# Three scatters behind each values step, and a wait for landings after each eighth

## What is computed

```python
x = x + _L0_xattn_ref(ctx_768, _layernorm(x, axis=-1), mask, ...)   # out = softmax(qn @ kn.T) @ v, then @ Wo.T + bo
x = x + _L0_ffn_ref(_layernorm(x, axis=-1), gate_w, gate_bias, w_gate, w_up, w_down)

# in _L0_ffn_ref, n = 4096 tokens, E = 64, K = 8, CAP = 256
scores = jax.nn.sigmoid(x @ gate_w.T)
topk_idx = jax.lax.top_k(tmp, K)[1]                       # tmp: scores + bias, within the best 4 groups
pos = jnp.take_along_axis(jnp.cumsum(oh, 0) - 1, e[:, None], 1)[:, 0]
buf = jnp.zeros((E, CAP + 1, h), x.dtype).at[e, pos_c].set(x[token])[:, :CAP]   # rows scattered to slots
g = jnp.einsum('ech,ehi->eci', buf, w_gate)
u = jnp.einsum('ech,ehi->eci', buf, w_up)
y = jnp.einsum('eci,eih->ech', jax.nn.silu(g) * u, w_down)
out = jnp.zeros((n, h), jnp.float32).at[token].add(y_slots * w_slot[:, None])
```

## Time and profile before

| | us |
|---|---|
| median of 3 runs | 1155.54 (1154.9 to 1157.93) |
| the profiled execution | 1165.68, its span 1163.8 |
| PE busy | 897.9 (77%) |
| VectorE busy | 660.5 (57%) |
| ScalarE busy | 463.1 (40%) |
| POOL busy | 616.1 (53%) |

### The profile page before, as it was taken

One profiled execution on the slowest core, in us unless ns is written; L12 is line 12 of the kernel. 1 busy time (PEld: TensorE's weight loads), 2 busy tenths in 40 slices (PEclk: granted clock), 3 DMA queues, 4 the chain that ended last, 5 costly groups with the idle time before them and its releaser, 6 DMA issues.

```text
span 1163.8 us, 13512 instructions
## 1 busy us (share of the span) xinstructions
PE 897.9 (77%) x3944; PEld 637.4 (55%) x3944; DVE 660.5 (57%) x1953; ACT 463.1 (40%) x931; POOL 616.1 (53%) x571
## 2 busy tenths in 40 slices
PE   2779999899999999989964974957209999888300
PEld 1445666556666657566642643856108888776200
DVE  4475657976888874978752644743623444333206
ACT  3834675645675546664530522422103333222000
POOL 4530323215766635755665063145555888888840
PEclk9969999989999999999985996968559999999655
DMA  7739601112222322101261102000518999898689
GB/s 249 269 100 386 232 5 53 38 31 105 80 73 76 125 68 88 65 7 68 79 230 65 37 28 88 24 23 9 205 67 252 308 313 182 160 162 138 71 237 385
DMA packets 85336, 150.79 MB, mean 130 GB/s; under 512 B 14089, under 2 KB 53049, under 8 KB 83215
## 3 DMA queue, kind: packets, MB, share of 16 engines
q1 hardware_dynamic: 54543, 112.32, 27.7%
q0 software_dynamic: 30720, 37.61, 16.3%
HBM read 69.19 MB, written 97.45 MB: 143 GB/s over the span
## 4 chain that ended last, share of the span: by engine, by line
PE 53%; DVE 13%; issue 10%; DMA 7%; POOL 6%; another core or an unknown queue 5%; ACT 5%; POOLq 0%; SPq 0%; DVEq 0%; ACTq 0%
PE ps_o L1302 15%; PE ps_u L1366 5%; PE ps_s L1278 4%; PE ps_u L1222 4%; PE ps_u L1192 4%; PE ps_s L1280 4%; POOL sum L1144 3%; DMA out_rows<-again,row_ids 3%; DVE mp L1637 3%; PE ps_o L1297 2%; PE ps_o L1375 2%; PE ps_u L1314 2%; POOL out_rows L1144 2%; DMA again<-out_rows 2%
## 5 line engine op out<-in xcount | busy, mean ns | idle before, releaser
L1069 POOL DMA_INDIRECT slot_rows<-rows,slot_idx x256 | 253.1, 989 | 237.9 <-issue 133.4
L1637 DVE TENSOR_REDUCE mp<-ps_u 128x1 f32<-128x512 f32 x256 | 165.1, 686 | 123.0 <-PE ps_u L1222 72.2
L1507 ACT ACTIVATE probs<-ps_s 128x512 f32<-128x512 f32 x256 | 139.8, 596 | 181.5 <-PE ps_s L1280 112.4
L1144 POOL DMA_INDIRECT sum<-again,row_ids x84 | 131.1, 1561 | 25.7 <-issue 22.0
L1302 PE MATMUL ps_o<-probs,pool 128*128 128x512 f32 (+1 forms) x288 | 138.0, 601 | 4.4 <-ACT den L1528 4.4
L1366 PE MATMUL ps_u<-again 128*128 128x256 f32 x512 | 122.3, 382 | 0.0
L1302 PE MATMUL ps_o<-probs,V 128*128 128x512 f32 (+1 forms) x216 | 105.6, 611 | 6.0 <-ACT probs L1510 4.3
L1280 PE MATMUL ps_s<-qbT,Kb 65*128 65x512 f32 (+1 forms) x252 | 102.5, 407 | 0.0
L1809 DVE TENSOR_SCALAR again<-ps_o,again 128x256 f32<-128x256 f32 x128 | 56.1, 480 | 77.3 <-DMA sum<-again,row_ids 46.4
L1366 PEld LDWEIGHTS ps_u<-again 128*128 128x128 f32 x512 | 93.2, 192 | 10.4
L1144 POOL DMA_INDIRECT out_rows<-again,row_ids x44 | 68.8, 1564 | 27.2 <-DVE row_ids L1810 14.3
(11 more groups left out here) (201 smaller groups left out, 1763.5 us busy)
## 6 DMA issues: line engine op xcount, KB each, us to landing
again<-in_wexp SPq DMA_DIRECT2D x64, 384.0 KB
slot_rows<-rows SPq DMA_DIRECT2D x2, 10272.0 KB, 35.0
again<-slot_rows SPq DMA_DIRECT2D x64, 321.0 KB
sum<-rows SPq DMA_DIRECT2D x2, 4352.0 KB, 27.9
again<-sum SPq DMA_DIRECT2D x8, 1024.0 KB, 11.5
Kb<-K SPq DMA_DIRECT2D x16, 275.5 KB
pool<-in_x SPq DMA_DIRECT2D x4, 1024.0 KB, 5.2
xres<-in_x SPq DMA_DIRECT2D x8, 512.0 KB
```

Of the source, the lines that this page charges most:

```text
L1069: pool.indirect_dma_start(out=slot_rows, out_offset=bass.IndirectOffsetOnAxis(ap=slot_idx[x][:, q, k:k + 1], axis=0), in_=rows[x][:, q, :] ...
L1144: pool.indirect_dma_start(out=(out, *sums)[e % PLANES], out_offset=bass.IndirectOffsetOnAxis(ap=row_ids[:, e % RING, t:t + 1], axis=0), in ...
L1507: act.activation(probs[:, n % NPR, hh, :], ps_s[:, u % NSC, :], ACT.Exp).then_inc(s["probs_made"], 1)
L1637: v.tensor_reduce(mp[:, i, tile, half:half + 1], bank((*t, i))[:, :], AX.X, ALU.max).then_inc(s["emptied_vec"], 1)
```

## The change

Batch 2 is given a start step for each half, `THREE_FROM`: step 107 for half 0 and step 119 for half 1. From there on three scatters go behind the values of each step: scatter n (0 to 31) of the half waits for step 107 + n // 3 or 119 + n // 3, with a wait instruction at each third. So the last scatters wait for the steps 117 and 129. For half (3, 0) the function `grouped` is true: before scatters 8, 16 and 24 POOL waits until all scatters before have landed. Half (3, 1) is as before. `paced` is used by the planner's simulation too.

```diff
+GROUP = 8
+THREE_FROM = {(B - 2, 0): 107, (B - 2, 1): 119}
...
         if (b, x) < (B - 2, 0):
             return NKT * PR * (2 * b + x + 2) + (TOPK * q + k) // 2
+        if (b, x) in THREE_FROM:
+            return THREE_FROM[(b, x)] + (TOPK * q + k) // 3
+
+    def grouped(self, b, x):
+
+        return (B - 2, 0) <= (b, x) < (B - 1, 1) and self.paced(b, x, 0, 0) is None
...
-                if plan.paced(b, x, q, k) and k % 2 == 0:
+                if plan.paced(b, x, q, k) and (TOPK * q + k) % (3 if (b, x) in THREE_FROM else 2) == 0:
                     pool.wait_ge(s["values_done"], plan.paced(b, x, q, k) + 1)
+                before = TOPK * q + k
+                if plan.grouped(b, x) and before and before % GROUP == 0:
+                    pool.wait_ge(s[f"scattered{x}"], HALF_SCATTERS * b + 16 * before)
```

## The result

The changed kernel takes 1111.72 us (median of 4 runs, 1109.37 to 1115.11); the kernel before took 1155.22 beside it (4 runs, 1149.77 to 1157.93). The ratio is 0.9613, 95% interval 0.959 to 0.9636: 43.5 us less. The forecast was 1119.5 with a range of 1095 to 1150. The profiled execution of after took 1109.89 us, that of before 1165.68.

The account below looks back on a forecast made before the run. It took the kernel to be PE bound except in four stalls from a backlog of POOL's back-to-back scatters. Terms 18 + 7 + 9 + 0 + 2 = 36 us off the 1155.5 median gave 1119.5, range 1095 to 1150.

Parts of the forecast that it names:

- The bound: Four stretches between 599 and 805 us: scatters 1.29 us apart build a backlog that stalls all engines; 1.56 can be digested.
- (a): Batch 2, half 0, from step 107: pacing saves 33 us of stall, loses 15 to slower steps; gain 18, bounds 0 and 33.
- (b): Batch 2, half 1, from step 119: 14 gained at the block change, less 2 and 5; net +7, bounds -4 and 25.
- The -5: Steps 126 to 129: the 11 scatters moved there cost 3.7 steps 1.4 us more each, 5 us lost.
- (c): Batch 3, half 0: landing waits, 0.9 us each, shorten the stalls of two bursts, +5 and +4; bounds 0 and 20.
- The slack: POOL's 10.39 us idle before half 1 of batch 3 (819.35) absorbs the landing waits' 2.6 us, so they cost nothing.
- The third rival: Moved scatters stall the last half, 11 us, and landing waits delay the last scatters, 5 us: +16, 1171 us; chance 0.11.
- (d): Residual addition on POOL ahead of 8 scatters: costs 0, or 2.78 us if the cover is gone.
- (e): PE's granted clock, 0.57 to 0.74 in the stalled windows: shorter idle stretches give back +2 us, between 0 and 6.
- the signs named beforehand: Steps 109 to 111 below 20 us, 125 to 126 under 20, no unowned piece over 8 before the tail, tail not growing.
- the stall outlives the pacing: First rival: three scatters per step pace nothing until PE is late; only -4 to -15 us, about 1145; chance 0.14.
- The lock between VectorE and POOL: Second rival: a shared SBUF port stalls by number of scatters, so no change, 1155 within 3.5 us; within the 0.08 chance.

Follow-up runs that it names:

- e1: Changed kernel with only half (2,0) paced from step 107, no pacing of (2,1) and no landing waits: 1149.84 us, ratio 0.9877 to the kernel before.
- e2: Changed kernel with only half (2,1) paced from step 119, no pacing of (2,0) and no landing waits: 1151.02 us, ratio 0.9905 to the kernel before.
- e3: Changed kernel with only the landing waits of half (3,0), no pacing by values: 1147.9 us, ratio 0.988 to the kernel before.
- e15: The changed kernel unaltered, run again on the third chip, which has no stall: 1094.48 us, ratio 1.0067 to the kernel before.
- e4: Changed kernel without pacing by values, landing waits at each eighth scatter of (2,0), (2,1), (3,0), stalling chip: 1107.93 us, ratio 0.9536 to the kernel before.
- e14: Landing waits at each eighth scatter of (2,0), (2,1), (3,0), no pacing by values, third chip without stall: 1093.04 us, ratio 1.0028 to the kernel before.
- e12: Kernel before with scatters of the last two batches writing 160 of 321 numbers per row to an unread table, third chip: 1091.18 us, ratio 1.0014.

## Why the prediction came out right, and where it did not

**The bound.** That the four stretches are stalls that go with back-to-back scatters, and that pausing POOL takes them away: right. e1, e2 and e3 each break up one of POOL's bursts and see the stall go or shrink at that place and stay elsewhere. The load of the expert weights, which falls in the first stall, isn't its cause: in 599 to 633 the DMA engines move 212 GB/s in after without a stall, 196 in before. The cause given, a backlog for which "1.56 us per scatter can be digested, 1.29 cannot", fits the runs on the stalling chips roughly: the long runs at 1.29 us stall, and the long stalls go when the runs are broken up. How many scatters it takes varies, though: the unowned piece begins at the 8th (599.45 after 590.31), the 12th (685.85 in e2) or the 15th (690.62 after 671.96, 661.36 after 643.06). The 9 scatters from 602.06 to 612.38 and the 7 from 688.97 pass, while eights have short pieces (732.33 and 746.89 in after). A backlog isn't shown, and rate, length of a run and bytes are not told apart, for want of the spacing and size runs on such a chip. The landings show no backlog: in the kernel with landings in three halves the first waits are as long on a stalling chip as on one without stalls, 6.91 and 6.94 us from the start of the eighth scatter to that of the ninth (593.89 to 600.80; 601.62 to 608.56). And the figures don't hold for other chips: on the two without stalls 21 whole rows at 1.29 us make no stall.

**(a), half (2,0).** +18 were forecast, 27.6 measured from step 107 to 111, less 2.3 lost from 111 to 117: 25. The step that failed is "3.87 us of POOL against 3.12 us of a step": 3.12 was read between 573 and 588, but steps 107 to 117 take 46.7 us without a stall, 4.67 each, since block work lies among them (9.6 us between 107 and 108 alone). Three scatters in 4.67 us are one per 1.56, just what the prediction held to be digestible. So these steps run as without a stall (24.6 us against 22.9 for 107 to 111), and the 15 us lost of (a) never came. By the same mistake the bound of 33 was too high: steps 109 to 111 take 10.2 us without a stall and not 6.24, so 29.3 could be won there, and 29.2 were. POOL's scatters of this half spread over 55.9 us (591.08 to 646.93), inside the 45 to 60 forecast.

**(b), half (2,1).** 14 at the change of block, less 2, less 5. Measured: 13.0 from step 124 to 126, -0.2 before it, and 0.0 in steps 126 to 134, where the 11 moved scatters now fall (688.97 to 703.84). So 12.8 where 7 were forecast. The -5 failed: POOL does run flat out there, but 7 scatters and then 4 bring no stall there, so they cost PE nothing. What is left here, 26.1 us against 17.6, is the stall at 661.36. It is where the prediction's words hold, that "while PE runs well POOL still runs flat out": the steps take 2.9 us, three scatters 3.87, and the waits are empty. e2 has the same stall (685.85, at the 12th of 18 scatters) with POOL in time, so the lateness behind (2,0) is not needed for it.

**(c), the landings of (3,0).** +5 and +4 forecast; 11.4 and 4.5 measured, with 1.6 lost between. The first burst's stall vanished altogether (13.9 us against 14.2 without a stall): the prediction had each half of the burst stall again, "only in its last two or three scatters plus the draining", which did not happen here. At the second burst a part is left, as it forecast: steps 140 to 142 take 13.7 us against 7.3 without a stall. The price of a wait was put at 0.9 us from the single landing of 2.13; it was 4.29 at 725.25, 5.27 us from the start of the last scatter at 719.98. At the same place it was 2.44 (3.43 from that start) in e3 on a stalling chip and 2.50 (3.49) in e15 on one without, so the difference isn't the chip's; what makes it is open. By the fit of the Trainium skill ("DMA: Bandwidth & Descriptors", section "Anatomy of one DMA — SWDGE (gpsimd) path") an estimate for one transfer of 164 KB is 2.0 + 0.4 = 2.4 us. The landing of the earlier trace rows (2.13) is near it; the 3.43 to 5.27 of the landings behind eight scatters are above it.

**The slack.** "So they cost nothing on the path" rested on POOL's 10.39 us of idle time. In after that idle time is 2.15 us (766.52), and in a trace without a stall it is 0.30, the gap between any two scatters in a row (before 754.03 in e15). So the slack was made by the stalls and went with them. On the profile's chip the waits still cost nothing that shows (the stretch from the last values to the last scatter is 54.6 us, against 56.8), since POOL waits for slot numbers later on (789.94); where there is no stall to gain from, the same waits are the 3.9 us by which POOL ends later. The third rival, slower because the landing waits use up POOL's slack, is therefore what happens on two of the chips, at 4 to 5 us and not at 16, under a condition that the prediction did not have: that there be no stall.

**(d), (e).** The addition at 633.17 has no wait before it, as forecast; its 2.79 us are part of POOL's lateness in (b). The clock was not measured apart: the stretches of the account hold it. In 599 to 633 it went from 0.63 to 0.98.

**The sum.** 36 us were forecast in the trace and 55.7 came; 36 were forecast in the medians and 43.5 came. That the forecast came to within 8 us is in part luck, two errors of opposite sign: the terms were 20 us short, and the profiled run of before was 10.5 us longer than its median. "The stall is hardly made by the profiler" was right, since the medians gain 43.5 us too. Most of the signs named beforehand came: steps 109 to 111 take 10.3 us, 125 to 126 17.0, no unowned piece is over 8 us, and the tail did not grow.

**The rivals.** That the stall outlives the pacing holds for one place only (7.14 us at 661.36). The lock between VectorE and POOL as the cause of the stalls falls: by it the time would not have moved, but with the same 256 scatters, of 991 ns each after as 989 before, it fell by 43.5 us.

After's page, the group that answers to the earlier trace rows:

```profile
L1080 POOL DMA_INDIRECT slot_rows<-rows,slot_idx x256 | 253.7, 991 | 199.4 <-issue 94.4
```

## What to carry to other kernels

When the other engines stand still at once while one issues transfers back to back, try breaking the runs up, by waiting for the landings of each eight or for another engine's progress. For the second read the length of a step where the waits stand, not elsewhere: three scatters a step paced POOL where a step takes 4.67 us and left it flat out where it takes 2.9. Idle time read in a stalled trace is not slack: work out who is last once the stall is gone. And run a remedy on more than one chip before it is kept: this one is worth 3.9% on a chip that stalls and costs 0.5 to 0.7% on one that does not.

## What the runs showed of the hardware that was not expected

- The stall comes and goes with the chip, or with the occasion: each group of runs was on a chip and at a time of its own, so the two can't be told apart. The same kernel before took 1155.22 and 1163.34 us in two groups of runs and 1090.29 and 1089.84 in two others, with no time between 1092.05 and 1149.77. The changed kernel took 1111.72, 1094.45 and 1094.48. In the traces without a stall the instructions, the 1.29 us between scatters and their 0.98 us are the same; only the other engines' waits aren't late. What differs between the groups no run here tells, nor whether the bytes, the number or the rate of the scatters make the stall: the runs made for that question all fell on chips without the stall.
- From the start of the last scatter of an eight to the start of the next, which waits for its landing, it takes 3.43 to 6.91 us with stalls (e3, e4, after) and 2.98 to 6.94 without (e14, e15). The last scatter of all lands after 2.13.
- POOL pauses about 2 us before the 29th scatter of each half in before and after (1.97 to 2.09; 709.85 before, 643.06 after), and in the traces without a stall as well (2.00 at 684.87 in e12). The prediction read the pause at 709.85 as what let the waits through. ScalarE's copy does start 1.92 us behind it, but the pause stands there without any stall too; why is open.
- A memset of 128 x 8 between two scatters lengthens the gap from 1.29 to 1.88 us, a second one only to 2.05.
